# Second stage's drain: the mixture's sum and second norm ahead of the masked maximum, the norm rows' transposes ahead of the values' products

## Time and profile before

| what | value |
|---|---|
| median of 3 executions | 988.67 us (986.96 to 990.8) |
| profiled execution, its own time | 987.03 us |
| its span, first to last instruction | 984.9 us |
| mean granted TensorE clock | 0.958 |
| PE busy | 900.4 us, 91% |
| DVE busy | 730.3 us, 74% |
| POOL busy | 551.4 us, 56% |
| ACT busy | 543.4 us, 55% |

### The profile page before, as it was taken

The page is one execution under the profiler, slowest core; times in us unless marked ns, Lnnn a source line. Parts: engine busy times, 40 slices in busy tenths (PEclk is TensorE's granted clock), DMA queues, the critical chain, the costliest instruction groups (busy, mean ns, idle before and its releaser), DMA issues. The chain is left out here.

```text
span 984.9 us, 31478 instructions
## 1 busy us (share of the span) xinstructions
PE 900.4 (91%) x10664; PEld 668.7 (68%) x10664; DVE 730.3 (74%) x2071; ACT 543.4 (55%) x1068; POOL 551.4 (56%) x897
## 2 busy tenths in 40 slices
PE   4799999999999999986999999999976399999993
PEld 2477777777777777754466666666644289889892
DVE  6688888888888888866778888888865356666773
ACT  3377777777777777654044444444443065555551
POOL 6655555565555555401037777777776535556536
PEclk9899999999999999987999999999996599999997
DMA  5644554445444454331565555665552348786535
GB/s 157 178 128 142 144 147 134 135 144 147 125 139 141 142 142 144 94 105 47 141 179 174 183 186 186 189 191 184 175 190 90 120 100 197 176 187 105 96 64 59
DMA packets 107278, 140.56 MB, mean 143 GB/s; under 512 B 23929, under 2 KB 92592, under 8 KB 106928
## 3 DMA queue, kind: packets, MB, share of 16 engines
q1 hardware_dynamic: 94594, 121.38, 41.3%
q0 software_dynamic: 12528, 17.18, 9.7%
HBM read 93.38 MB, written 38.35 MB: 134 GB/s over the span
## 5 line engine op out<-in xcount | busy, mean ns | idle before, releaser
L999 DVE TENSOR_REDUCE smax<-psum 112x2 f32<-112x750 f32 x240 | 216.3, 933 | 24.5 <-PE psum L439 24.4
L840 ACT ACTIVATE probsT<-psum 125x896 f32<-125x896 f32 x173 | 158.7, 917 | 22.0 <-PE psum L454 20.6
L2035 POOL DMA_INDIRECT out_dram<-y,token_at x63 | 101.6, 1612 | 93.9 <-DMA out_dram<-y,token_at 42.2
L1733 DVE SCALAR_TENSOR_TENSOR acc<-psum,neg_bias,acc 128x448 f32<-128x448 f32 x112 | 75.9, 680 | 10.9 <-PE psum L1556 9.3
L1475 POOL DMA_INDIRECT dispatch_dram<-rows,slots_at x64 | 64.0, 1000 | 28.4 <-issue 28.4
L439 PE MATMUL psum<-k_stack,q_stack 63*128 63x375 f16 x480 | 69.3, 326 | 3.9 <-DVE smax L999 2.8
L1556 PE MATMUL psum<-xT_hi,we_hi 128*128 128x448 f16 x256 | 70.2, 356 | 1.1 <-ACT we_hi L1655 1.1
L476 PE MATMUL psum<-probsT,v_aug 125*32 125x112 f32 x2688 | 70.2, 260 | 0.1
L1556 PE MATMUL psum<-xT_lo,we_hi 128*128 128x448 f16 x256 | 69.8, 355 | 0.0
L1556 PE MATMUL psum<-xT_hi,we_lo 128*128 128x448 f16 x256 | 69.7, 354 | 0.0
L476 PEld LDWEIGHTS psum<-probsT,v_aug 125*32 125x32 f32 x2688 | 63.5, 110 | 8.9 <-ACT v_aug L866 8.5
(11 more groups left out here) (298 smaller groups left out, 2448.3 us busy)
## 6 DMA issues: line engine op xcount, KB each, us to landing
k_stack<-k_hi_dram SPq DMA_DIRECT2D x64, 188.0 KB, 2.8
we<-in_ctxT_dram SPq DMA_DIRECT2D x32, 375.0 KB, 3.5
ctxT<-in_ctxT_dram SPq DMA_DIRECT2D x32, 375.0 KB
ctx_rows<-in_ctx_dram SPq DMA_DIRECT2D x32, 375.0 KB
w_raw<-in_w_dram SPq DMA_DIRECT2D x32, 256.0 KB, 3.9
rows_e<-dispatch_dram SPq DMA_DIRECT2D x24, 272.0 KB
k_hi_dram<-k_hi SPq DMA_DIRECT2D x32, 188.0 KB, 2.8
k_lo_dram<-k_lo SPq DMA_DIRECT2D x32, 188.0 KB, 2.7
```

Source lines behind the costliest of these rows:

```text
L840: nc.scalar.activation(probsT[:, p, c, hg, :, :, :].rearrange("p k h q -> p k (h q)"), psum[0:KC, 0:2, 0:4 * S], ACT.Exp, scale=float(HD) ...
L999: nc.vector.reduce_max(smax[:, (u - LAG_B) % 2, 2 * (s % 4) + s // 4::PAIRS], psum[0:S, pair_bank(s):pair_bank(s) + 2, 0:KV], AX.X).then_i ...
L1733: nc.vector.scalar_tensor_tensor(out, psum[:, mix_bank(t, u, k), 0:GT], neg_bias[:, hc, e:e + 1], out, ALU.max, ALU.add).then_inc(m["acc_r ...
L2035: nc.gpsimd.indirect_dma_start(dram["out"], bass.IndirectOffsetOnAxis(token_at[:, unit // PAIR % TOKEN_TURNS, unit % PAIR:unit % PAIR + 1] ...
```

## The change

In the drain steps that have part `a` (`a and not f`), three engines get another order; all other steps keep theirs. DVE does the sum and the second norm's statistics ahead of the masked maximum and its bias. ACT writes `x2n` straight behind the exponential, then the copy of the turned probabilities, then the weight cast. PE turns `x2n` ahead of the values' products. POOL and SP keep their order. The unused nested function in `attention_phase` goes.

```diff
@@ attention_phase, tensor
-
-            def maxima_turned(b):            run_steps(pe, step)
@@ middle_phase, tensor, step
                 mix(2)
+                def rows_turned():
+                    wait(pe, m["x2n_rdy"], cnt(t, ua, 1, 1))
+                    for kc in range(DC):
+                        last = nc.tensor.transpose(psum[:, 2, D + kc * S:D + (kc + 1) * S], x2n[:, kc * 128:(kc + 1) * 128], ident[0:S, 0:S])
+                    last.then_inc(m["x2nT_done"], 1)
+
+                if a and not f:
+                    rows_turned()
                 if o:
                     wait(pe, rows_in[uo % 2], loads(t, uo))
...
                     last.then_inc(m["o_done"], 1)
-                if a:
-
-                    wait(pe, m["x2n_rdy"], cnt(t, ua, 1, 1))
-                    for kc in range(DC):
-                        last = nc.tensor.transpose(psum[:, 2, D + kc * S:D + (kc + 1) * S], x2n[:, kc * 128:(kc + 1) * 128], ident[0:S, 0:S])
-                    last.then_inc(m["x2nT_done"], 1)
+                if a and f:
+                    rows_turned()
                 mix(3)
@@ middle_phase, scalar, step
+                def norm_rows():
...
+                def probs_turned():
...
+                if a and not f:
+                    norm_rows()
+                    probs_turned()
                 if a:
...
                     nc.scalar.activation(w_hi[:, bass.ds((t * TURN + ua) * W_PIECE, W_PIECE)], w_raw[:, ua % 2, :], ACT.Copy).then_inc(m["w_hi_rdy"], 1)
+                if o and (f or not a):
+                    probs_turned()
+                if a and f:
+                    norm_rows()
@@ middle_phase, vector, step
-                if o:
+                def masked_scores():
...
-                if a:
+                def second_norm():
...
+                draining = not f
+                if a and draining:
+                    second_norm()
+                if o:
+                    masked_scores()
+                if a and not draining:
+                    second_norm()
```

More of the change, by code:

```diff
@@ L1663, in step @@
                                          accum_out=prob_sum[:, uo % 2, :]).then_inc(m["exp_rdy"], 1)
-                if a:
-                    wait(act, m[f"w_in{ua % 2}"], loads(t, ua))
-                    apart(act)
-                    nc.scalar.activation(w_hi[:, bass.ds((t * TURN + ua) * W_PIECE, W_PIECE)], w_raw[:, ua % 2, :], ACT.Copy).then_inc(m["w_hi_rdy"], 1)
-                if o:
[L1670 to L1673, removed]
+                def norm_rows():
                     xrow = x_res[:, bass.ds(t * TURN + ua, 1), :].rearrange("p o d -> p (o d)")
@@ L1678, in step @@
                     nc.scalar.activation(x2n[:], xrow, ACT.Identity, bias=ln_shift[:, 0, :], scale=ln_rstd[:, 0, :]).then_inc(m["x2n_rdy"], 1)
+                def probs_turned():
+                    wait(act, m["pT_done"], cnt(t, uo, 1, 1))
+                    wait(act, m["o_done"], cnt(t, uo - 1, 1, 1))
+                    nc.scalar.activation(probsT[:].rearrange("p c s -> p (c s)"), psum[0:KC, 5, 0:NKC * S], ACT.Copy).then_inc(m["pT_rdy"], 1)
+                if a and not f:
+                    norm_rows()
+                    probs_turned()
+                if a:
+                    wait(act, m[f"w_in{ua % 2}"], loads(t, ua))
+                    apart(act)
+                    nc.scalar.activation(w_hi[:, bass.ds((t * TURN + ua) * W_PIECE, W_PIECE)], w_raw[:, ua % 2, :], ACT.Copy).then_inc(m["w_hi_rdy"], 1)
+                if o and (f or not a):
+                    probs_turned()
+                if a and f:
+                    norm_rows()
                 if k:
```

## The result

Slower: 995.55 us (median of 5 executions, 993.52 to 997.33) against 988.32 us for the kernel before (5 executions in the same comparison, 986.96 to 990.8), ratio 1.0072, interval 1.005 to 1.0094. The forecast was 991.2 with 994.8 as its upper end; of the rivals C, which said 995.2, lies nearest.

What follows compares the result with a forecast made beforehand. Order and waits were taken to bound the drain, POOL's 7.85 us chain setting the full-clock pace. Steps 0 to 3 summed 1.4 + 0.3 + 0.3 + 1.6 = +3.6 us; between median + 1.2 and + 3.6: 991.2 us, range 987.0 to 994.8.

Steps and rivals of the forecast that it cites:

- C: Drain: the 4.7 us gap drops one more step to half clock, 2.9 us more, 995.2 us; chance 0.17.
- What bounds the drain: Drain steps 0 to 3: no engine full, order and waits decide; POOL's chain of 7.85 us sets the pace at full clock.
- The delays: Drain steps: masked maximum 1.69 us later, values' products 1.82 us later, PE's gap from scores to products 2.9 to 4.7 us.
- The term at full clock: Drain steps at full clock: delayed products exceed their 1.58 us cover by 0.24 us, taken as 0.3 a step.
- The clock of steps 1 and 2: Drain steps 1 and 2: summed at full clock, +0.3 us each; losing that clock was left to a rival of chance 0.17.
- The rule of the Trainium skill: PE in the drain: transposes don't count as matmuls for the clock gate, idle gaps are risky; steps 1 and 2 could lose full clock.
- Rival B: Drain: products, third transposes and scores in one block keep step 3 at full clock, 2.6 us gained, 986.1 us; chance 0.10.
- Rival D: Drain: POOL's 7.85 us chain stays the bound, products just fit their cover, nothing changes, 988.7 us; chance 0.20.
- The expert stage: Stage after the drain, starting from the table: should have its old length.

Runs made afterwards that it cites:

- filled kernel before: Kernel before plus spare matmuls into an unread bank in PE's idle drain gaps: 984.52 us, ratio 0.9995; with more up to the expert stage: 984.29 us, 0.9994.
- filled kernel after: Changed kernel plus 14 spare matmuls a drain step ahead of the turned probabilities: 982.43 us, ratio 0.9978; repeated with more executions: 982.88 us, 0.9970.
- second profile: Changed kernel run again unchanged, against the kernel before: 994.78 us, ratio 1.0092; the kernel before, also profiled again unchanged, took 988.33 us.
- unfilled halves: Changed kernel without spare matmuls, keeping only DVE's swap: 995.85 us, ratio 1.0101; keeping only ACT's and PE's part: 994.88 us, ratio 1.0092.

## Why the prediction was wrong

*What bounds the drain*: right at full clock. POOL's queue at 7.85 us is the pace, and in steps 1 to 3 it has no idle time ahead of the second norm in the filled kernel before and the filled kernel after either. In the changed kernel as it stands it isn't the bound: POOL waited 1.55 us.

*The delays*: right. The maximum came 1.8 us later against the scores (2.00 us behind their end instead of 0.21), and the gap from scores to products was forecast at 4.7 us and measured at 4.70.

*The term at full clock*, 0.24, taken as 0.3 a step: too large. Measured 0 to 0.06 (7.83 to 7.90 against 7.84). It put the third transposes behind the modelled end of the products and the scores 0.33 us behind these. Running through, the transposes start 1.36 us after the products' start, 0.16 ahead of that end, and the scores 0.27 later: 1.63 us and not 1.85.

*The clock of steps 1 and 2* is the step that failed: "steps 1 and 2, which held full clock before", were summed at full clock, and their loss was left to rival C with 0.17. From scores to scores the kernel after took 9.15, 9.23, 8.77 and 10.78 us against 8.02, 7.79, 7.84 and 8.11: +1.1, +1.4, +0.9, +2.7, where the text had +1.4, +0.3, +0.3, +1.6. From the last scores to the table it took 1.0 less, because the clock came back before step 4: scores of 2.22 us and turned probabilities of 0.58 there instead of 2.82 and 0.97. That is 5.2, and in the second profile 8.5, where 3.6 were forecast. C's mechanism is the right one and its figure is near in part by luck: it has 3.6 + 2.9 = 6.5 us in the drain and nothing in the expert stage, from one more step that falls, where in both profiles all four steps fell, the drain lost 5.2 us (8.5 in the second), and the expert stage took 2.8 more. The gap of 2.9 us with two falls in four steps was the warning in the rows; making it 4.7 should have had the larger chance, since a gap that long was in every step.

*The rule of the Trainium skill*: its warning of idle gaps between bursts (TensorE: Matmul & The Clock Gate, Why this matters for your kernels) was the right side of the argument, and I gave it too little weight: in step 2 PE's longest stretch of standing still grew from 1.22 to 2.99 us. The Trainium skill's other statement, that transposes don't count as matmuls do (TensorE: Matmul & The Clock Gate, Part 4: PE-mode transpose), doesn't agree with the runs: 12 spare transposes a step left two falls in four steps (and 7 matmuls of the same time two as well), where without either there were four. Each of these counts is from one profile of four steps, or two for the four falls.

*Rival B* asked for full clock through step 3; with the clock held by other means such a gain is real: 54.9 to 55.1 us for the drain against 57.7. But the old order has it too once it is filled (55.20 and 54.99 us), so it is the clock's gain and not the order's. *Rival D* is what the change would be at full clock.

*The expert stage* "should have its old length": it had 2.8 us more, and 2.8 more again in the second pair of profiles (207.8 against 205.0). Windows of its start, from the table on, before and after:

```profile
775.60:800.00 24.40, 15.94 (x120) 13.05 (x121) 6.51 (x15) 8.70 (x19) 9.36 (x9) 0.76 0.31 92
```

```profile
779.30:804.00 24.70, 16.25 (x98) 12.40 (x99) 5.33 (x12) 7.23 (x15) 7.72 (x8) 0.65 0.31 91
```

The clock came back later (mean 0.76 and 0.65). Over all 14 profiles its length lies between 201.9 and 207.8 us: 204.1 and 205.0 for the kernel before, 206.9, 207.8, 206.5 and 203.3 for the changed one and its unfilled halves, 201.9 to 205.7 for the filled ones. Whether the drain's end shifts it or its own start does, these runs don't settle. With the drain's 5.2 and 8.5 us the measured 7.2 (and 8.9 in the second comparison) is accounted for to within that scatter.

## What to carry to other kernels

In a stretch where an engine has slack, moving its work later isn't free if that engine is TensorE: add up the longest stretch without its matmuls (transposes aside) before and after, and if the old one already cost a fall of the clock here and there, price the new one at half clock in every step. Here products and scores behind a pause of 4.7 us or more ran slower than behind one of 2.9, whether the norm rows' transposes stood between them or not. When an order is right for the dependences but lets the clock of TensorE fall, spare matmuls in the pause can turn a loss (1.0072) into a small gain (0.9970); they have to fit the pause, and with half of them two of four falls stayed. Fill the old order as well before the new one gets the credit: here the old one, filled, had as short a drain.

## What the runs showed of the hardware

- Spare transposes (float32, 128x128, 12 in 1.5 us) kept the granted clock up as often as 7 spare matmuls did: two falls in four steps with either, in one profile each, against four without.
- The pattern of the clock in a fixed program can repeat closely: the kernel before showed 0.79, 1.00, 1.00 and 0.67 in its four steps in both profiles. The changed one didn't: 0.81, 0.82, 0.82, 0.61 and 0.68, 0.68, 0.67, 0.60.
- Back to back, the values' products, two transposes, two rank products and the start of the scores take 1.63 us; with PE idle between products and transposes the last part alone took 0.33 instead of 0.27.
